# Two-attention kernel in FP32, first batch: the G projection ahead of its bias, A's parts ahead of the second half of xn, the first x over two queues

## The reference

```python
h = group_norm(x) * gn_w + gn_b                     # 32 groups
q, k, v = conv1x1(h, wq, bq), conv1x1(h, wk, bk), conv1x1(h, wv, bv)
w = softmax(q^T k / sqrt(256))                      # 1024 x 1024 for each batch
x1 = x + conv1x1(w applied to v, wo, bo)
att = x1 x1^T; att_c = softmax(max(att) - att)      # channels, 256 x 256
fb, fc, fd = conv1x1(x1, wb), conv1x1(x1, wc), conv1x1(x1, wd)
att_s = softmax(fb^T fc)                            # 1024 x 1024 again
out = (beta * att_c x1 + x1) + (alpha * fd att_s + x1)
```

## Time and profile before

| what | value |
|---|---|
| median of 3 runs | 452.03 us |
| lowest, highest | 449.42, 454.62 us |
| the profiled execution | 454.26 us |
| its span in the profile | 452.3 us |
| PE busy | 427.1 us, 94% of the span |
| VectorE, ScalarE, GpSimd busy | 328.3, 292.5, 58.1 us |

### The profile page before, as it was taken

The page is one execution under the profiler, slowest core; times in us unless marked ns, Lnnn a source line. Parts: engine busy times, 40 slices in busy tenths (PEclk is TensorE's granted clock), DMA queues, the critical chain, the costliest instruction groups (busy, mean ns, idle before and its releaser), DMA issues.

```text
span 452.3 us, 5951 instructions
## 1 busy us (share of the span) xinstructions
PE 427.1 (94%) x2078; PEld 355.3 (79%) x2078; DVE 328.3 (73%) x491; ACT 292.5 (65%) x368; POOL 58.1 (13%) x52
## 2 busy tenths in 40 slices
PE   2899999999999999999999999999999997887995
PEld 2798887888888878879888888878888875665874
DVE  3537877866789988778888686787878675698621
ACT  1425584768767776778666666778667665868520
POOL 1400040013000510210002310400000014001000
PEclk9879999999999999999999999999999999999999
DMA  7612647442066586540744446540955454047631
GB/s 227 212 68 46 112 77 185 91 96 48 0 115 119 103 224 133 104 90 15 218 94 93 79 90 138 114 94 23 194 109 102 92 133 94 0 95 138 144 90 46
DMA packets 140396, 48.03 MB, mean 106 GB/s; under 512 B 135824, under 2 KB 137296, under 8 KB 140368
## 3 DMA queue, kind: packets, MB, share of 16 engines
q1 hardware_dynamic: 136400, 36.52, 42.0%
q0 software_dynamic: 2144, 7.34, 4.5%
q10 hardware_dynamic: 1824, 3.80, 2.5%
HBM read 9.90 MB, written 4.19 MB: 31 GB/s over the span
## 4 chain that ended last, share of the span: by engine, by line
PE 86%; DVE 5%; DMA 3%; issue 2%; ACT 2%; POOL 1%; SPq 0%; POOLq 0%; ACTq 0%; DVEq 0%
PE sum_ps L739 13%; PE sum_ps L741 13%; PE sum_ps L740 13%; PE score_ps L739 12%; PE score_ps L741 12%; PE score_ps L740 12%; PE score_ps L851 2%; PE score_ps L881 2%; DMA x<-in_L_conv_wo_dram 2%; DVE pieces L624 2%; PE score_ps L749 1%; DVE negmax L608 1%; POOL xn_l L349 1%; PE score_ps L861 1%; DMA land<-pieces 1%
## 5 line engine op out<-in xcount | busy, mean ns | idle before, releaser
L416 ACT ACTIVATE exps<-score_ps,negmax 128x1024 f32<-128x1024 f32 x64 | 71.2, 1112 | 47.4 <-DVE negmax L608 33.8
L624 DVE SCALAR_TENSOR_TENSOR pieces<-exps,recip,pieces 128x1024 f16<-128x1024 f32 x64 | 82.7, 1296 | 13.1 <-ACT pieces L426 12.5
L437 ACT ACTIVATE pt_h<-land 128x1024 fp32r<-128x1024 f16 x64 | 66.5, 1055 | 34.6 <-PE sum_ps L741 27.3
L608 DVE TENSOR_REDUCE negmax<-score_ps 128x1 f32<-128x1024 f32 x64 | 77.3, 1218 | 13.0 <-PE score_ps L741 7.5
L426 ACT ACTIVATE pieces<-exps,recip 128x1024 f16<-128x1024 f32 x64 | 72.9, 1142 | 15.7 <-DMA land<-pieces 10.1
L635 DVE TENSOR_SCALAR pt_l<-land 128x1024 fp32r<-128x1024 f16 x64 | 51.9, 824 | 20.7 <-PE sum_ps L741 20.3
L739 PE MATMUL sum_ps<-pt_h,v_h 128*128 128x512 f32 x160 | 62.8, 393 | 0.6 <-DVE x L711 0.6
L741 PE MATMUL sum_ps<-pt_h,v_l 128*128 128x512 f32 x160 | 62.4, 390 | 0.0
L740 PE MATMUL sum_ps<-pt_l,v_h 128*128 128x512 f32 x160 | 62.3, 390 | 0.0
L739 PE MATMUL score_ps<-xn_h,g_h 128*128 128x512 f32 x128 | 50.7, 396 | 0.1
L741 PE MATMUL score_ps<-xn_h,g_l 128*128 128x512 f32 x128 | 50.0, 390 | 0.0
(11 more groups left out here) (148 smaller groups left out, 777.5 us busy)
## 6 DMA issues: line engine op xcount, KB each, us to landing
out_dram<-x POOLq DMA_DIRECT2D x16, 256.0 KB, 2.9
x_in<-in_x_dram POOLq DMA_DIRECT2D x6, 512.0 KB, 4.3
x<-in_x_dram ACTq DMA_DIRECT2D x6, 512.0 KB, 4.5
x_in<-in_x_dram SPq DMA_DIRECT2D x2, 512.0 KB, 4.4
x<-in_x_dram SPq DMA_DIRECT2D x2, 512.0 KB, 4.5
land<-pieces SPq DMA_TRANSPOSE x64, 4.4
x<-in_L_conv_wk_dram ACTq DMA_DIRECT2D x1, 256.0 KB, 4.0
x<-in_L_conv_wo_dram SPq DMA_DIRECT2D x1, 256.0 KB, 7.4
```

The source lines that it names most:

```text
L416: act.activation(exps[:, n % 2, :], score_ps[s][:, :], ACT.Exp, bias=negmax[:, n % RING:n % RING + 1], scale=1.0, accum_out=rowsum[:, n % ...
L437: act.activation(pt_h[:, at:at + 2, :], land[:, k % 2, 0, t:t + 2, :], ACT.Copy, scale=1.0 / PIECE)\
L608: dve.tensor_reduce(negmax[:, n % RING:n % RING + 1], score_ps[s][:, :], AX.X, ALU.max, negate=True)\
L624: dve.scalar_tensor_tensor(pieces[:, n % 2, 1, :], exps[:, n % 2, :], recip[:, n % RING:n % RING + 1], pieces[:, n % 2, 0, :], ALU.mult, A ...
```

## The change

1. PE_ORDER begins with G.0.0, BG, V.0.0, W instead of BG, G.0.0, W, V.0.0. ACT_ORDER and DVE_ORDER take V.0.0's parts before W's.
2. In the prologue ScalarE and VectorE make xn's first column half, then the parts of A (and ScalarE the copy of A), and only then xn's second column half and the parts of B.
3. The second half of the first x is loaded by ScalarE's queue, ahead of wk, instead of by SyncE's behind the first half.
4. In the lists a few finishing steps of the sums and their stores (fx, fo, st) swap their two channel halves.

```diff
-    BG G.0.0 W V.0.0 S0.0.0 MEAN.1 S0.0.1 S0.0.2 VAR.1 S0.0.3 G.0.1 V.0.1 S0.0.4 S0.0.5 S0.0.6 S0.0.7 O0.0.0x6
+    G.0.0 BG V.0.0 W S0.0.0 MEAN.1 S0.0.1 S0.0.2 VAR.1 S0.0.3 G.0.1 V.0.1 S0.0.4 S0.0.5 S0.0.6 S0.0.7 O0.0.0x6
...
-    bn.1 lG.0.0 lW lV.0.0 max0.0.0 spread.1 r0.0.0 max0.0.1 b0.0.0 max0.0.2 gvar.1 r0.0.1 r0.0.2 max0.0.3 b0.0.1
+    bn.1 lG.0.0 lV.0.0 lW max0.0.0 spread.1 r0.0.0 max0.0.1 b0.0.0 max0.0.2 gvar.1 r0.0.1 r0.0.2 max0.0.3 b0.0.1
...
-            for m in range(CH):
-                sp.dma_start(x_in[:, m, :], x_dram[0, :, m, :]).then_inc(x0_loaded[m], 16)
+            sp.dma_start(x_in[:, 0, :], x_dram[0, :, 0, :]).then_inc(x0_loaded[0], 16)
...
+            act.dma_start(x_in[:, 1, :], x_dram[0, :, 1, :]).then_inc(x0_loaded[1], 16)
             act.dma_start(wk_sb, wk.rearrange("(m p) c -> p m c", p=P)).then_inc(wk_loaded, 16)
...
+            xn0_high(0)
+            act.wait_ge(gn_w_loaded, 16)
+            weight_high(a_ps, a_w, a_full, a_high)
+            act.wait_ge(a_made, 1)
+            act.activation(a1_sb, rows_of(a_ps), ACT.Copy).then_inc(a_copied, 1)
+            xn0_high(1)
+            weight_high(b_ps, b_w, b_full, b_high)
+            act.wait_ge(b_made, 1)
+            act.activation(b1_sb, rows_of(b_ps), ACT.Copy).then_inc(b_copied, 1)
...
+            xn0(0)
+            for m in range(CH):
+                dve.wait_ge(xn_high, m + 1)
+                last = low(xn_l[:, m, 0:QC], x_in[:, m, 0:QC], xn_h[:, m, 0:QC])
+            last.then_inc(x0_low, 1)
+            dve.wait_ge(gn_w_loaded, 16)
+            weight_low(a_ps, a_w, a_high, a_made)
+            xn0(1)
+            weight_low(b_ps, b_w, b_high, b_made)
```

More of the change, by code:

```diff
@@ L35 @@
 ACT_ORDER = """
-    ldx1.1 hG.0.0 hW hV.0.0 exp0.0.0 a0.0.0 exp0.0.1 exp0.0.2 a0.0.1 a0.0.2 hG.0.1 exp0.0.3 hV.0.1 a0.0.3
+    ldx1.1 hG.0.0 hV.0.0 hW exp0.0.0 a0.0.0 exp0.0.1 exp0.0.2 a0.0.1 a0.0.2 hG.0.1 exp0.0.3 hV.0.1 a0.0.3
     exp0.0.4 exp0.0.5 a0.0.4 cvh.0 cvh.2 xnh.1.0 xnh.1.1 cvh.4 exp0.0.6 a0.0.5 cvh.6 a0.0.6 exp0.0.7 hG.1.0
@@ L58 @@
 DVE_ORDER = """
-    bn.1 lG.0.0 lW lV.0.0 max0.0.0 spread.1 r0.0.0 max0.0.1 b0.0.0 max0.0.2 gvar.1 r0.0.1 r0.0.2 max0.0.3 b0.0.1
+    bn.1 lG.0.0 lV.0.0 lW max0.0.0 spread.1 r0.0.0 max0.0.1 b0.0.0 max0.0.2 gvar.1 r0.0.1 r0.0.2 max0.0.3 b0.0.1
     xn.1.0 b0.0.2 lG.0.1 r0.0.3 lV.0.1 xn.1.1 b0.0.3 max0.0.4 max0.0.5 r0.0.4 r0.0.5 max0.0.6 cvl.0 cvl.2 b0.0.4
-    max0.0.7 cvl.4 r0.0.6 cvl.6 b0.0.5 b0.0.6 r0.0.7 lG.1.0 bn.2 b0.0.7 max0.1.0 fx.0.0.0 max0.1.1 fx.0.0.1
+    max0.0.7 cvl.4 r0.0.6 cvl.6 b0.0.5 b0.0.6 r0.0.7 lG.1.0 bn.2 b0.0.7 max0.1.0 fx.0.0.1 max0.1.1 fx.0.0.0
     r0.1.0 max0.1.2 cvl.8 b0.1.0 spread.2 cvl.10 r0.1.1 max0.1.3 cvl.12 b0.1.1 gvar.2 cvl.14 r0.1.2 r0.1.3
-    xn.2.0 xn.2.1 b0.1.2 fx.0.1.1 fx.0.1.0 b0.1.3 lV.1.0 lXT.0.0 lV.1.1 lXT.0.1 cvl.16 cvl.18 lFBC.0 lG.1.1 sA.0
+    xn.2.0 xn.2.1 b0.1.2 fx.0.1.0 fx.0.1.1 b0.1.3 lV.1.0 lXT.0.0 lV.1.1 lXT.0.1 cvl.16 cvl.18 lFBC.0 lG.1.1 sA.0
     max2.0.0 max2.0.1 r2.0.0 r2.0.1 cvl.20 lFD.0.0 b2.0.0 aA.0 max2.0.2 b2.0.1 max2.0.3 cvl.22 r2.0.2 minE.0
@@ L66 @@
     cvl.24 cvl.26 max0.1.7 r0.1.6 b0.1.5 max2.0.4 b0.1.6 cvl.28 max2.0.5 r0.1.7 cvl.30 r2.0.4 b0.1.7 max2.0.6
-    r2.0.5 b2.0.4 lG.2.0 max2.0.7 cvl.32 fo.0.0.1 fo.0.0.0 cvl.34 b2.0.5 r2.0.6 max0.2.0 r2.0.7 max0.2.1 cvl.36
+    r2.0.5 b2.0.4 lG.2.0 max2.0.7 cvl.32 fo.0.0.0 fo.0.0.1 cvl.34 b2.0.5 r2.0.6 max0.2.0 r2.0.7 max0.2.1 cvl.36
     b2.0.6 bn.3 b2.0.7 cvl.38 max0.2.2 r0.2.0 r0.2.1 b0.2.0 fx.1.1.0 fx.1.1.1 cvl.40 cvl.42 max0.2.3 r0.2.2
@@ L75 @@
     r0.3.1 r0.3.2 b0.3.1 max0.3.3 cvl.72 cvl.74 r0.3.3 lV.3.0 cvl.76 b0.3.2 b0.3.3 cvl.78 lFBC.2 lXT.2.0
-    max2.2.0 lXT.2.1 cvl.80 r2.2.0 fo.1.1.1 lG.3.1 max2.2.1 fo.1.1.0 cvl.82 lV.3.1 b2.2.0 r2.2.1 sA.2 b2.2.1
+    max2.2.0 lXT.2.1 cvl.80 r2.2.0 fo.1.1.0 lG.3.1 max2.2.1 fo.1.1.1 cvl.82 lV.3.1 b2.2.0 r2.2.1 sA.2 b2.2.1
     max0.3.4 aA.2 max2.2.2 cvl.84 r0.3.4 minE.2 max2.2.3 cvl.86 b0.3.4 r2.2.2 nE.2 max0.3.5 b2.2.2 r2.2.3 r0.3.5
@@ L87 @@
 POOL_ORDER = """
-    ldxin.1 rstd.1 xnl.1.0 xnl.1.1 ldxin.2 rstd.2 x1l.0.0 x1l.0.1 xnl.2.0 xnl.2.1 ldxin.3 st.0.0.1 st.0.0.0
-    x1l.1.0 x1l.1.1 st.0.1.1 st.0.1.0 rstd.3 xnl.3.0 xnl.3.1 st.1.0.1 st.1.0.0 x1l.2.0 x1l.2.1 st.1.1.1 st.1.1.0
+    ldxin.1 rstd.1 xnl.1.0 xnl.1.1 ldxin.2 rstd.2 x1l.0.0 x1l.0.1 xnl.2.0 xnl.2.1 ldxin.3 st.0.0.0 st.0.0.1
+    x1l.1.0 x1l.1.1 st.0.1.1 st.0.1.0 rstd.3 xnl.3.0 xnl.3.1 st.1.0.1 st.1.0.0 x1l.2.0 x1l.2.1 st.1.1.0 st.1.1.1
     st.2.0.1 st.2.0.0 x1l.3.0 x1l.3.1 st.2.1.0 st.2.1.1 st.3.0.0 st.3.0.1 st.3.1.1 st.3.1.0
@@ L379, in _, with xn0_high, weight_high @@
             act.activation(wot_sb, rows_of(sum_ps[0][:, :]), ACT.Copy).then_inc(wot_made, 1)
[L380 to L384, removed]
+            def xn0_high(c):
+                for m in range(CH):
+                    act.wait_ge(xn_made, c * CH + m + 1)
+                    high(xn_h[:, m, cols(c, QC)], x_in[:, m, cols(c, QC)]).then_inc(xn_high, 1)
+            def weight_high(ps, w, full, staged):
                 act.wait_ge(full, 1)
@@ L389, in _ @@
                 last.then_inc(staged, 1)
-            for ps, plain, made, copied in ((a_ps, a1_sb, a_made, a_copied), (b_ps, b1_sb, b_made, b_copied)):
-                act.wait_ge(made, 1)
-                act.activation(plain, rows_of(ps), ACT.Copy).then_inc(copied, 1)
+            xn0_high(0)
[7 more added lines that the diff above has]
+            act.activation(b1_sb, rows_of(b_ps), ACT.Copy).then_inc(b_copied, 1)
             def rest():
@@ L565, in _, with xn0, weight_low @@
             dve.wait_ge(rstd_made, 1)
-            for c in range(CHUNKS):
+            def xn0(c):
                 for m in range(CH):
                     normalised(m, cols(c, QC)).then_inc(xn_made, 1)
[L569 to L574, removed]
+            def weight_low(ps, w, staged, made):
                 dve.wait_ge(staged, 1)
```

## The result

The changed kernel takes 454.61 us (median of 20 runs, 453.43 to 455.48), the kernel before 452.23 (20 runs, 449.42 to 454.78). The ratio is 1.0051 with an interval of 1.0029 to 1.0073: 0.5% slower. The prediction was 451.2 with a range up to 453.3, so it had the wrong sign. The profiled execution of the changed kernel took 454.54 us, its span is 452.6. The runs of before lie in three heaps, at about 449.5, 452.1 and 454.5; the changed kernel never comes under 453.4. It has lost the low executions.

The account below looks back on a forecast made before the run. PE, busy 94% of the span, was taken as the bound, through S0.0.0's start: 4.2 us earlier less 1.7 lost clock, net 2.5, profiled 454.26 to 451.8; median forecast 451.2 against 452.03, range 449.2 to 453.3.

Parts of the forecast that it names:

- The start: Loads and statistics ahead of A: splitting the first x gains 0.3 us; bounds 0.5 later to 0.8 earlier.
- later weights: Bound for the start of A: weights in ScalarE's queue slip behind half of x, A 0.5 us later.
- G ahead of its bias, the gap gone: PE behind B: G.0.0 follows at once, removing the 1.46 us gap; with the start, PE's row moves 1.76 earlier.
- The new limit: S0.0.0 waits for lG behind bn.1 and batch 1's load, landing at 25.9; S0.0.0 begins at 28.6 to 28.7.
- the rival of the late load: Batch 1's load lands later than 26.3, holding S0.0.0 and making the kernel slower: 453.0 us; chance 0.17.
- a full shift: Late bound for batch 1's second half: landing slips 2.2 us along with GpSimd's later issue, to 27.3.
- The clock in S0.0.0: After PE's wait, 3.4 us at half clock lose 1.7 us in S0.0.0; bounds nothing and 2.5.
- The step to the median: From 449.2 for full-clock runs: 450.1 without lost clock, 451.8 with 1.7 lost; median taken as 451.2.
- nothing differs behind 60 us: Rest of the program: PE should not lose or win more than 1 us there.
- The rival on the other side: Batch 1's load replaces the gap: lands at 27.3, lG ends at 30.0, 453.0 us, 1 us slower; chance 0.17.

Follow-up runs that it names:

- e2: Changed kernel with only the split of the first x undone (both halves on SyncE's queue); 454.32 us, ratio 1.0055.
- e4: Kernel before with only the split of the first x over two queues; 452.47 us, ratio 1.0003.
- e8: Changed kernel with ScalarE's load of batch 1 (ldx1.1) moved behind G.0.0's high part; 451.43 us, ratio 0.9997.
- e5: Kernel before with the new prologue order, old first orders, one queue for x, and the fx, fo, st swaps; 453.44 us, ratio 1.0036.
- g1: e1 with 10 extra 512-column matmuls in PE's wait ahead of FBC.3 (378 us); 449.30 us, ratio 0.9947.
- f1: Changed kernel with 12 extra 512-column matmuls in PE's wait ahead of S0.0.0; 452.14 us, ratio 1.0015.
- e1: Changed kernel with batch 1's statistics (bn.1) moved behind lG.0.0 and lV.0.0 on VectorE; 449.82 us, ratio 0.9959.
- e7: Kernel before with bn.1 moved behind lG.0.0 and lW on VectorE; 452.03 us, ratio 0.9996.
- e3: Changed kernel with only the prologue's order undone (all of xn ahead of A's and B's parts); 451.48 us, ratio 0.9985.

## Why the prediction was wrong

- **The start, 0.3 us earlier: wrong in sign.** A began at 10.58 and not at about 10.06. The second half of x no longer came late, but the gn_w row did, behind it: VectorE's product with wk waited for it until 8.64, and VAR and A stand behind the small steps that follow. wq, for which I had worked out the bound, landed 0.4 us earlier than before (9.7). I had named later weights as one bound and let equal bytes decide. The rule of the Trainium skill that I weighed there (DMA: Bandwidth & Descriptors, Issuing engines are not separate DMA queues) leaves only an issue to be saved, which the earlier trace rows put at 0.4 us; that nothing more was to be had agrees with e2 and e4, where the split cost 0.3 at A. That both halves came together, at 5.6, the first 1.3 later than before, agrees with the turns between queues of the same page (section Queues, rings and completion order).
- **G ahead of its bias, the gap gone: right.** PE went from B into G.0.0 at 16.72 (16.0 forecast; A began 0.5 later than forecast), at full clock, BG took 1.84, V.0.0 about 3, and W ended at about 27.3 (26.5).
- **The new limit: right in its place, wrong in its size.** This is the step that failed: "I take 25.9" for the landing of the second half. It landed at 27.7, 1.8 later, beyond the 26.3 at which I had put the turning point of the rival of the late load and beyond my own bound of a full shift, 27.3. The rest of the term held: statistics of 1.29 and g_l of 1.39 behind it, S0.0.0 at 30.40 instead of 28.7. Two things were wrong in it. Both issues came later than I had them, GpSimd's at 20.36 (19.8 forecast) and ScalarE's at 19.63 (18.6 forecast; it comes after ScalarE's copy of B, which slipped by 1.5 us and not by 0.5), so the sum of bytes itself ended later: 25.2 before, 27.7 now, for a first issue at 17.53 and at 19.63. And I took the load that goes first as the one that fills the engines for both; it filled them for itself, and GpSimd's half was the last of all to land. e8 shows that this order was worth 1.8 us at S0.0.0.
- **The clock in S0.0.0: right.** 1.7 us forecast; it took 4.2 us (30.40 to 34.60) where before it took 2.8 (32.86 to 35.63), so 1.4 lost. That the loss comes "wherever the wait falls" was too strong: e5 stands 1.38 us ahead of S0.0.0 and keeps its clock, and g1 loses it there without a wait.
- **The step to the median: right for the lowest run, once S0.0.0 is put right.** I had 449.2 us plus what S0.0.0 stands later than 27.8, plus the clock. With 30.4 and 1.4 in it this gives 449.2 + 2.6 + 1.4 = 453.2, and the lowest run is 453.43. In other kernels it comes within 0.4 us as well: f1's profile, without half clock and with S0.0.0 at 30.8, took 451.87 (452.2 by the rule), e1's lowest run, with S0.0.0 at 27.1, took 448.44 (448.5). The heaps of the kernel before are about what I took them for: its profile at 454.26 holds 10.2 us of half clock, that of e7 at 451.96 holds 6.8, and each lost half of it; 449.2 and 448.6 remain, where the lowest runs are 449.42 and 449.56. I had put the median of the changed kernel at 451.2, between 450.1 without the lost clock and 451.8 with it; that placing is 0.6 of the miss.
- **What I hadn't costed: half clock late in the program.** The median lies 1.2 us above the lowest run, so of the 3.4 us that the forecast missed this is the second part, beside the 1.7 at S0.0.0 and the 0.6 of the placing. In the profiled execution PE was 1.45 us ahead at FBC.3 (380.46 against 381.91), and lost 3.4 us in the two stretches near 382 and 402, of which later waits gave some back; the span ended 0.3 us longer. I had written that nothing differs behind 60 us. The waits that precede these stretches are the same in the kernel before, where its profiled execution kept its clock. Why one execution loses it there and another doesn't is left open, and so is how many of the runs do.
- **The rival on the other side was the case.** "The load of batch 1 takes the place of the gap" gave S0.0.0 at 30.0 and 453.0, within 0.4 us of what came at S0.0.0 and 1.6 under the median. It had 0.17. e1 shows its mechanism, e5 that it outweighs the gap that was removed. My argument against it, that the other load comes first and the bytes are shared, is in truth the argument for it.

## What to carry to other kernels

Before work is pulled ahead on one engine, ask what now stands later on the others and which transfer's issue waits for that; here 0.8 us of PE's row was bought with an issue 2.8 us later of a load whose consumer stood, in strict order, ahead of G's own low part. Where two loads share the engines, the sum of bytes tells only when the last piece of both lands; whose piece that is, their order of issue decided here (e8, and e3 the other way round from the changed kernel). And a statistic of the next batch is better placed behind what the current one waits for: that one move (e1) turned the slower kernel into a faster one.

## What the runs showed of the hardware

- A load issued by GpSimd 0.7 us behind ScalarE's, both 1.05 MB, got hardly a share until the other was nearly through: from 21 to 23 us no packet of GpSimd's queue moved and ScalarE's had 97.9% of the engines' time. The Trainium skill, DMA: Bandwidth & Descriptors, section Queues, rings and completion order, says that an engine takes turns between the queues that have work for it. The row doesn't look like turns, though, going by e8, GpSimd's queue had work by then: there, with its load issued at the same time and ScalarE's behind it, it moved 0.30 MB in the same two us (first row). Issued 0.6 us ahead of ScalarE's, in the kernel before, it did share: from 22 to 24 us both moved about the same (the other two rows). What decides between the two is left open. Issued ahead, its halves landed 4.0 and 6.8 us after their issues; issued behind, 6.1 and 6.6. In e7, with ScalarE's load 0.5 us ahead, that load was again in first, both halves by 21.7, and GpSimd's at 23.0 and 24.2.

```profile
q0 software_dynamic: 74, 0.30, 60.9%
...
q0 software_dynamic: 109, 0.44, 54.3%
q10 hardware_dynamic: 91, 0.36, 44.4%
```

- Runs of one unchanged kernel lay in three heaps, 2.4 to 2.6 us apart. In the profile of before the half clock at the start accounts for the distance from the lowest run within 0.3 us; in that of e7 it takes 1.0 us too much. Why the heaps stand 2.5 us apart, when one stretch of the profiles is worth 1.7, stays open. In the changed kernel a wait of 3.06 us on PE was followed by 1.4 us lost to half clock, and filling it with useless matmuls took 2.5 us off the median.
